# Gathered rows as three bfloat16 pieces, 88 blocks by matrix, and a round at every fourth step with four places left out

## The reference

```python
Xs = X[src]
msg = jnp.where((edge_types == 0)[:, None], Xs @ W_data.T + b_data, Xs @ W_control.T + b_control)
agg = jax.ops.segment_sum(msg, dst, num_segments=X.shape[0])
out = jax.nn.relu(agg + (X @ W_self.T + b_self))
result = _layernorm(x + out, axis=-1)      # all float32
```

## Time and profile before

| | us |
|---|---|
| median of 3 runs (3984.35 to 3987.94) | 3986.37 |
| the profiled execution | 3988.85 |
| its span on the core | 3987.1 |
| PE matmul busy | 2650.9 (66%) |
| POOL busy | 1715.3 (43%) |
| DVE busy | 1623.9 (41%) |
| ACT busy | 1267.6 (32%) |
| mean granted PE clock | 0.816 of full |

### The profile page before, as it was taken

The page is one execution under the profiler, slowest core; times in us unless marked ns, Lnnn a source line. Parts: engine busy times, 40 slices in busy tenths (PEclk is TensorE's granted clock), DMA queues, the critical chain, the costliest instruction groups (busy, mean ns, idle before and its releaser), DMA issues.

```text
span 3987.1 us, 50434 instructions
## 1 busy us (share of the span) xinstructions
PE 2650.9 (66%) x19115; PEld 1498.6 (38%) x19115; DVE 1623.9 (41%) x3683; ACT 1267.6 (32%) x2283; POOL 1715.3 (43%) x1815
## 2 busy tenths in 40 slices
PE   3566676666766677666666666667666666767666
PEld 2333343333433344333333334334333333333334
DVE  7434344334443344434344343434334343443332
ACT  4233232333323333333333333333333333323332
POOL 6434444344443444444344443444444344444432
PEclk9878788888887888888787888878888787888878
DMA  5111111111111111111111111111111111111110
GB/s 163 50 32 34 35 32 37 32 36 35 34 36 32 36 34 37 34 34 36 33 36 34 34 35 34 35 35 34 36 34 36 32 36 34 34 37 31 37 34 26
DMA packets 112877, 151.17 MB, mean 38 GB/s; under 512 B 35545, under 2 KB 82712, under 8 KB 112632
## 3 DMA queue, kind: packets, MB, share of 16 engines
q0 software_dynamic: 58432, 119.78, 11.4%
q1 hardware_dynamic: 54200, 28.09, 2.5%
HBM read 138.99 MB, written 8.76 MB: 37 GB/s over the span
## 4 chain that ended last, share of the span: by engine, by line
another core or an unknown queue 39%; PE 36%; ACT 17%; issue 6%; DVE 1%; DVEq 0%; DMA 0%; SPq 0%; ACTq 0%
PE apply_ps L615 20%; ACT cnt L799 15%; PE sum_ps L581 6%; PE build L599 5%; PE misc L664 2%; PE misc L667 1%; PE misc L665 1%; PE misc L666 1%; ACT sg L782 1%; ACT std L824 0%; ACT zg L784 0%; PE misc L558 0%; DVE cnt L1074 0%; DVE hot_q L1063 0%
## 5 line engine op out<-in xcount | busy, mean ns | idle before, releaser
L517 POOL DMA_INDIRECT rows<-in_x,src_t x1760 | 1670.9, 949 | 2195.0 <-PE sum_ps L581 1694.1
L615 PE MATMUL apply_ps<-x,cnt 128*128 128x385 bf16 x8428 | 1753.4, 364 | 10.4 <-issue 10.3
L799 ACT ACTIVATE cnt<-build 128x784 bf16<-128x784 f32 x1376 | 1060.9, 817 | 1878.0 <-remote 1586.2
L599 PE MATMUL build<-hot_q,hot_p 64*128 64x196 bf16 x5504 | 452.8, 274 | 1226.0 <-ACT cnt L799 1104.6
L615 PEld LDWEIGHTS apply_ps<-x,cnt 128*128 128x128 bf16 x8428 | 908.9, 110 | 686.9 <-issue 294.3
L599 PEld LDWEIGHTS build<-hot_q,hot_p 64*128 64x128 bf16 x5504 | 194.3, 97 | 1509.8 <-issue 1338.4
L1063 DVE TENSOR_TENSOR hot_q<-const_ps,key_pq 128x784 bf16<-128x784 f32 x688 | 663.4, 964 | 0.0
L1063 DVE TENSOR_TENSOR hot_p<-const_ps,key_pq 128x512 bf16<-128x512 f32 x688 | 468.4, 681 | 134.4 <-remote 108.5
L1135 DVE SCALAR_TENSOR_TENSOR y_sb<-misc,x_u 128x128 f32<-128x128 f32 (+2 forms) x104 | 30.3, 292 | 1057.4 <-PE misc L667 896.6
L1108 DVE TENSOR_TENSOR acc_deg<-misc,acc_deg 2x32 f32 x352 | 63.1, 179 | 927.5 <-PE misc L624 652.4
L782 ACT ACTIVATE sg<-sum_ps 128x129 f32<-128x129 f32 x176 | 49.0, 279 | 774.2 <-PE sum_ps L581 758.1
(11 more groups left out here) (174 smaller groups left out, 1063.5 us busy)
## 6 DMA issues: line engine op xcount, KB each, us to landing
rows<-in_x,src_t POOLq DMA_INDIRECT x1760
cnt<-in_x SPq DMA_DIRECT2D x13, 448.0 KB
x_u<-in_x SPq DMA_DIRECT2D x42, 64.0 KB
out<-out_sb SPq DMA_DIRECT2D x42, 64.0 KB
key_dram<-fin SPq DMA_DIRECT2D x12, 192.0 KB
x_u<-in_x SPq DMA_DIRECT2D x40, 53.5 KB
out<-out_sb SPq DMA_DIRECT2D x40, 53.5 KB
win_i<-in_dst SPq DMA_DIRECT2D x22, 64.0 KB, 2.0
```

The costliest lines, as they stand in the source:

```text
L517: pool.indirect_dma_start(out=rows[:, slot, 0:D], out_offset=None, in_=x, in_offset=bass.IndirectOffsetOnAxis(ap=src_t[:, col:col + 1], ax ...
L599: last = pe.matmul(build_ps[z][:, o:o + 2 * XBLOCKS], hot_p[half, slot, :], hot_q[half, slot, :], start=True, stop=True)
L615: last = pe.matmul(apply_ps[:, 0:385], cnt[:, k % 2, b, :], x3[:, b, 0:385], start=(b == 0), stop=(b == XBLOCKS - 1))
L799: act.activation(o, i.rearrange("p h (m b) -> p b h m", b=XBLOCKS), ACT.Copy).then_inc(evacuated, 1)
```

## The change

- `BLOCKS` goes from 86 to 88. 704 steps now build, where 688 did, and the last `apply` is in step 711. 1730 tiles are left to gather, which is 173 rounds.
- The rounds keep a grid of four steps, with 177 places, from step 0 to step 704. Places 23, 67, 111 and 155 have no round. The steps of the other jobs are now found by `place(s)`, which takes the next free step. So 70 of the units' outputs lie in the last step of a group of four (63 before), 24 turns of a unit's x lie there too (none before), and the loop ends 14 steps later.
- From round 12 (`F32_ROUNDS`) on, POOL gathers from a new DRAM tensor `x3_dram`, whose rows are the three bfloat16 pieces: 768 bytes instead of 512. PE adds them up with ten bfloat16 matmuls of 385 columns, one instruction each, and DVE adds the three pieces (`add_parts`), in place of ACT's `take_sums`.
- ACT's queue stores `x3` to `x3_dram` in steps 6 to 12, with 15 DMAs (`store_x3`).
- `AHEAD` goes from 3 to 2 rounds (`SLOTS` 20): the gathers of round r + 2 begin when round r is done.
- The last units have 88 rows instead of 128.

```diff
-BLOCKS = 86
+BLOCKS = 88
-GATHER_0 = 1365
+GATHER_0 = 1395
-SLOTS = 30
-AHEAD = 3
+SLOTS = 20
+F32_ROUNDS = 12
+ROW = 3 * D
+AHEAD = 2
...
+    places = (BATCHES + APPLY_AT) // 4 - (0 if BLOCKS == 86 else 1)
+    spare = places - PAIRS
+    left_out = {2 * ((places * (2 * i + 1) // (2 * spare)) // 2) + 1 for i in range(spare)}
+    gather_step = [4 * j for j in range(places) if j not in left_out][:PAIRS]
...
+    def place(s):
+        while s in taken:
+            s += 1
+        taken.add(s)
+        return s
+
+    sum_step = [place(s + 1) for s in gather_step]
+    key_step = {g: place(32 * g - 8) for g in range(1, KGROUPS)}
+    ptr_step = {g: place(8 if g == 1 else 32 * (g - 1)) for g in range(1, KGROUPS)}
+    block_step = [place(APPLY_AT + 8 * k + 10) for k in range(BLOCKS)]
...
+        x3_dram = nc.dram_tensor("x3_dram", [N, ROW], BF16).ap()
-        rows = sb("rows", [P, SLOTS, 132])
+        rows = sb("rows", [P, SLOTS, ROW + 2], BF16)
...
+                if ps == F32_ROUNDS:
+                    pool.wait_ge(x3_stored, 16 * (XCH + 1))
...
+                        out=rows_f[:, slot, 0:D] if early else rows[:, slot, 0:ROW],
+                        out_offset=None, in_=x if early else x3_dram,
...
-                    last = pe.matmul(sum_ps[64 * g:64 * g + 64, 0:D + 1], hot[:, ps % 3, g * GT + j, :],
-                                     rows[:, slot, 0:D + 1], start=(j == 0), stop=(j == GT - 1))
+                    part, st = slice(64 * g, 64 * g + 64), g * GT + j
+                    if ps < F32_ROUNDS:
+                        last = pe.matmul(sum_ps[part, 0:D + 1], hot[:, ps % 3, st, :], rows_f[:, slot, 0:D + 1],
+                                         start=(j == 0), stop=(j == GT - 1))
+                    else:
+                        last = pe.matmul(sum_ps[part, 0:ROW + 1], hot_b[:, ps % 3, st, :], rows[:, slot, 0:ROW + 1],
+                                         start=(j == 0), stop=(j == GT - 1))
...
+            def store_x3(c):
+
+                full = XB if c < XCH - 1 else XB - 1
+                act.wait_ge(x3_ready, c + 1)
+                act.dma_start(x3_dram[c * XB * P:(c * XB + full) * P, :].rearrange("(b p) d -> p b d", p=P),
+                              x3[:, c * XB:c * XB + full, 0:ROW]).then_inc(x3_stored, 16)
...
-                if q == 0 and ps < PAIRS:
-                    take_sums(ps)
+                if gather_at.get(s, PAIRS) < F32_ROUNDS:
+                    take_sums(gather_at[s])
...
+                for c in (2 * s - 12, 2 * s - 11):
+                    if 0 <= c < XCH:
+                        store_x3(c)
...
+            def add_parts(ps):
+
+                dve.wait_ge(rows_used, ps + 1)
+                dve.tensor_tensor(zg[:, ps % 2, :], t_mask[:, 0, :], sum_ps[:, ROW:ROW + 1].to_broadcast([P, 2]),
+                                  ALU.mult)
+                dve.tensor_reduce(sg[:, ps % 2, 0:D], sum_ps[:, 0:ROW].rearrange("p (k d) -> p d k", k=3), AX.X,
+                                  ALU.add).then_inc(sg_ready, 1)
```

More of the change, by code:

```diff
@@ L40 @@
 XB = 7
-TAIL = 4
 FIRST_X = 5
@@ L74, in gnn_resnorm @@
         cut = [n0 + (n1 - n0) * i // k for i in range(k + 1)]
+        end = sum_step[min(EPOCH * (e + 1), PAIRS) - 1]
         for i in range(k):
[L76 to L81, removed]
+            t, o = ((9, 10), (11, 15), (19, 23))[i]
+            wanted.append((end + t, Unit(cut[i], cut[i + 1] - cut[i], end + t, end + o, False, e % 2, cut[i] - base)))
+    tail_wanted = [w for w in wanted if w[1].n0 == DENSE - P or w[0] >= sum_step[-1] + 5 and not w[1].dense]
+    ends = [w[1] for w in tail_wanted]
+    TAIL = len(ends)
+    assert TAIL == 4 and ends[0].dense and not any(v.dense for v in ends[1:])
+    units = []
+    for s, v in sorted((w for w in wanted if w not in tail_wanted), key=lambda w: w[1].out):
+        s = place(max(s, units[-1].turn + 1 if units else 0))
+        units.append(v._replace(turn=s, out=place(max(s + 1, v.out, units[-1].out + 1 if units else 0))))
+    assert all(b.turn > a.out for a, b in zip(units, units[2:]))
     UNITS = len(units)
@@ L85, in gnn_resnorm @@
     assert len(turn_at) == UNITS and len(out_at) == UNITS
[L86 to L107, removed]
+    for v in units:
+        if not v.dense:
+            e = (v.n0 - WIN_0) // EPOCH_NODES
+            assert e + 2 >= EPOCHS or v.out + 2 < sum_step[EPOCH * (e + 2) - 1]
+        else:
+            u = v.n0 // P
+            assert v.out < block_step[min(2 * u + 4, BLOCKS - 1)]
+    TURN_END = BATCHES + 3
+    STEPS = max(taken) + 4
+    gather_at = {s: r for r, s in enumerate(gather_step)}
+    sums_at = {s: r for r, s in enumerate(sum_step)}.get
+    keys_at = {s: g for g, s in key_step.items()}.get
+    ptr_at = {s: g for g, s in ptr_step.items()}.get
+    block_turn_at = {s: k for k, s in enumerate(block_step)}.get
+    hot_at = {gather_step[r - 2] + 2: r for r in range(2, PAIRS)}
+    epoch_at = {sum_step[EPOCH * (e + 1) - 1] + 1: e for e in range(EPOCHS - 1)}
+    key_round = {min(r for r in range(PAIRS) if gather_step[r] >= s + (12 if g == 1 else 16)): g
+                 for g, s in ptr_step.items()}
     def posted_at(s):
@@ L137, in key_job @@
     def key_job(g):
-        return 1 if g == 0 else job[32 * g - 8]
+        return 1 if g == 0 else job[key_step[g]]
     def ptr_job(g):
-        return 0 if g == 0 else job[8 if g == 1 else 32 * (g - 1)]
+        return 0 if g == 0 else job[ptr_step[g]]
     ctx = ExitStack()
@@ L777, in split_mid @@
                 last.then_inc(mid_ready, 1)
+            def store_x3(c):
[3 more added lines that the diff above has]
+                              x3[:, c * XB:c * XB + full, 0:ROW]).then_inc(x3_stored, 16)
+                if full < XB:
+                    act.dma_start(x3_dram[(XBLOCKS - 1) * P:N, :], x3[0:XLAST, XBLOCKS - 1, 0:ROW]
+                                  ).then_inc(x3_stored, 16)
             def take_sums(ps):
@@ L874, in _ @@
                     act.wait_ge(end_turned, 1)
-                    act.activation(end_xt, build_ps[0][:, 0:TAIL * P].rearrange("p (j r) -> p j r", r=P),
-                                   ACT.Copy).then_inc(end_xt_ready, 1)
+                    for j, v in enumerate(ends):
+                        last = act.activation(end_xt[:, j, 0:v.r], build_ps[0][:, j * P:j * P + v.r], ACT.Copy)
+                    last.then_inc(end_xt_ready, 1)
             act.wait_ge(end_mv_ready, 1)
@@ L1193, in _ @@
                     post(posted_at(s))
+                if F32_ROUNDS <= gather_at.get(s, 0):
+                    add_parts(gather_at[s])
                 if sums_at(s) is not None:
```

115 lines of the change are left out of this document (67 added, 48 removed).

## The result

| | kernel before | changed kernel |
|---|---|---|
| median of 4 runs, us | 3986.89 (3984.35 to 3987.94) | 3943.68 (3940.96 to 3947.14) |
| ratio | 1 | 0.9894 (95%: 0.9882 to 0.9907) |
| span of the profiled execution, us | 3987.1 | 3939.8 |
| granted clock, mean | 0.816 | 0.825 |

The time fell by 43 us where the forecast was 12. The experiments then ran on three chips, and the kernel before took 3987, 3848 and 2310 us on them. They are called chips A, B and C here. The two kernels of the table ran beside each other, and as the kernel before took what it takes on A, they are counted to A. Times of kernels are compared only where both ran on the same chip.

A forecast was written before the change was run, and what follows sets the result against it. A serial loop through POOL, ACT and PE was taken as the bound, gathers holding back PE's signals to ACT. Terms +4 - 53 + 24 + 13 = -12 us gave 3974 us from 3986.4, 0.3% faster; range 3925 to 4070.

The forecast's parts named there:

- The frame: New schedule's beginning, held rounds, unheld round, left-out places and end, without the loop's own changes: together +4 us.
- Beginning, intervals and the unheld round: Round 5's sum at about 149: -13 us; one held interval fewer: -22.6; one more round without gathers behind it: +11.8.
- Left-out places: Four places without a round, each four steps with neither gathers nor sums, 10.5 us each: +42 us.
- The end: After the last sum, 19 us of applies and a 22 us finish, with the sum 42 us instead of 56.2: -14.
- The sums: PE's ten bfloat16 matmuls take 0.99 us instead of 1.32, -0.33 in each of 161 rounds: -53 us.
- the matmuls pair: Forecast: bfloat16 matmuls start in pairs on output halves. Rival: they don't, +80 instead of -53, 4107 us, chance 0.07.
- The larger gathers: 768-byte rows land later and release ACT later after POOL's last gather: +0.15 us a round, +24 us, bounds 0 and +48.
- ACT's freed 0.6 us: ACT's time freed by moving the sums' addition to DVE lies during POOL's gathers: no gain.
- The moved jobs: Seven more unit outputs behind the release, 1.86 us each: +13 us, bounds 0 and +25.
- The clock: Rival: PE's low clock after idling absorbs the loop's savings and costs, leaving only +4: 3990 us, chance 0.15.
- The larger transfers: Rival: larger gathers lengthen the hold of PE's signals by 0.7 us a round instead of 0.15: 4063 us, chance 0.10.
- let another step through: Rival: the hold catches another PE step; one more through, about 3590 us, one less, about 4380; chance 0.05 each.

The follow-up runs named there:

- the busy ACT: Changed kernel with ACT again waiting for the sums and running two small copies from round 12: 0.9965 of before on B, 2324.9 us (1.0065) on C.
- the kernel with float32 rows: Changed kernel, but all 173 rounds gather float32 rows and sum them with 20 float32 instructions: 4012.7 us on A, 1.0061 of before.
- the paced kernels: Changed kernel with waits added between POOL's gathers, all ten gathers kept: ratios to before from 0.7484 to 0.8784 on A and B, 1.1665 and 1.2827 on C.
- five gathers: Changed kernel, but from round 12 POOL gathers only five of ten sets of rows, each multiplied twice: 2652.7 us on A, 0.6651 of before.
- two bursts: Changed kernel, but POOL waits before the sixth gather until ACT has copied both halves of the third step's counts: 3162.4 us on A, 0.7931 of before.
- one each: Changed kernel, but from the third gather on each waits for one more half step's counts copied by ACT: 2982.5 us on A, 0.7484 of before.
- rows of three: Changed kernel, but POOL waits before every third gather until the previous one has landed: 3377.4 us on B, 0.8784 of before.

## Why the forecast was right in sign and short in size

**The bound.** The serial loop through POOL, ACT and PE was read rightly for this chip: on A, taking gathers away or breaking their row took 4.7 to 8.0 us out of each round with the same work on PE. That it is PE's signals that are late is borne out by the other waits: "remote" also ends waits of DVE for PE (122.9 us for `acc_deg` in the changed kernel), and none of PE's own. "If the hold were gone, PE's own steps would be next" is half shown on C: four steps take 12.56 us, where I had said 11.82, and POOL's 12.84 us a round stand beside them.

**The frame.** Beginning, intervals and the unheld round came within 2 us of their terms. Left-out places cost 11.4 us on average, not 10.5, as two of the four took 12.6. The end was -23 and not -14: after the last sums the applies took 19.6 us (I had 19), but the finish behind them 13.3 where I had carried 22 over from the earlier trace rows, which still held work of the last rounds.

**The sums.** Right: 1.01 us for ten, -53 in all, and the matmuls pair: 1.01 is 4 * 0.165 + 0.33 and a rounding, not 1.82. That rival is out.

**The larger gathers: the step that failed.** I had read from the earlier trace rows, a round that ends with key gathers, that 768 bytes release ACT 0.15 us later, and multiplied it by 161. On average the release comes 2.05 us after the last gather's end in the changed kernel, 2.02 in the same schedule with rows of 512 bytes, and 2.16 before (133, 133 and 137 rounds without key gathers). So the larger rows make a difference of 0.03 us there, and the 2.48 of that row wasn't the price of its bytes. One round is no price when the rows of 160 can be averaged. The landing did become later: the first event comes 2.34 us after a gather's start, 2.21 with 512 bytes, medians of over 1400 gathers each. The Trainium skill ("DMA: Bandwidth & Descriptors", Anatomy of one DMA, SWDGE path) fits a transfer with a fixed time and its bytes at 436 GB/s; an estimate by this page is 0.075 us more for the added 32 KB, and the trace has 0.13. But no one on the path waits for a landing here, and so neither figure belongs into the sum. Without this term, and with the finish at 13, the forecast would have been -12 - 24 - 9 = -45. That this is what was measured is luck: the lost pairs (+12) and the dearer places and unheld round (+5) had no term, and the 17 us that the gathers and moved jobs came out below +13 cancel them.

**ACT's freed 0.6 us.** I put them at nothing, as they lie beside the gathers. Between 13 and 27 us of the gain may be theirs or the clock's (the experiment with the busy ACT leaves it open; the traces lean to the clock).

**The moved jobs.** +13 forecast, +14 read from the kernel with float32 rows, but as a sum of +30 and -16.

**The rivals.** The clock didn't take the loop's savings back: float32 rows cost 69 us, more than the 53 of the sums. The larger transfers didn't lengthen the hold. No round let another step through more often; on the contrary, the pairs of the earlier trace rows were lost, 12 us which no term of mine had. The beginning was at 148.89, so x3's stores didn't press on it.

**What no rival had.** Each one was a number on the same chip. On C, where nothing is held, the same change makes the kernel 0.7% slower (1.0054 to 1.0081). An estimate for it from the lines above: 161 * 0.33 = 53 us less of sums, and 16 more steps of at least 2.5 us, 40 to 47 us more, comes out at about even; the measured +16 isn't explained, as no trace of the kernel before exists from C.

## What to carry to other kernels

Where an engine's wait has no releaser in the trace, ask which other engine's activity starts and ends with it, and break that activity up before tuning around it: one added wait a round in POOL's queue was worth 20%, eight were worth 24% of the changed kernel's time, where the whole change was worth 1.1%. Take a price from the mean over all its occurrences, not from the one row that shows it best. And before such a wait is kept, run both kernels on another chip: the paced kernels took 12 to 25% less time than the kernel before on A and B, while on C pacing cost 17 to 28% (by other waits than on A and B), and the unpaced kernel before was the fastest of all.

## What the runs showed of the hardware that I hadn't expected

- **A hold of PE's signals by gathers, on some chips only.** The kernel before took 3987.2 us on A, 3847.9 on B (13 runs, 3834.9 to 3857.1) and 2309.7 on C (9 runs, 2308.8 to 2310.8). Of the `build` signals to ACT from the 61st on, 164 of 1348 came over 3 us late in the changed kernel on A (168 of 1316 before), and none over 1 us late on C.
- **When it begins and ends.** In the kernels on A with unbroken rows of ten, signals raised up to 3.5 us after a row's first gather went through, and those from 5.3 us on were held (163 to 165 in each kernel); hardly any fall between. In "five gathers", "two bursts" and "one each" all but two of the held ones were raised after 3.6 us, and none after 4.6 us went through at once. The fourth gather of a row starts at 3.76 us. The release comes later behind a longer row: 1.1 us after the last of four gathers, 1.4 of five, 1.5 of six and 2.1 to 2.2 of ten (medians). A row of three doesn't start the hold: in that kernel 5 of 1348 signals were over 1 us late. An interruption of 1.7 us between two gathers mostly ends it.
- **The trace itself is thinner where signals are held.** It holds 9194 landing events of DMAs in the kernel before and 8801 in the changed one on A, 20896 with rows of three on B, and 31101 for the changed kernel on C, though from the changed kernel on the DMAs are the same. So the path that carries such events may be what is congested; that is a guess. The Trainium skill ("NOTIFIC — Programmer's Manual", 1.1 The problem) says of the recording of events: "The engine never blocks on the host". Its section 1.2 (The design, and what it trades) names modes in which a full ring loses records or stalls the producer. The missing events would fit the first of these; whether recording has a part in the hold, no run here shows, since all of them were recorded.
- **A landing has a beginning and an end.** A gather's first event comes at 2.34 us, but a wait for all sixteen ends 2.90 to 2.92 us after its start on B. A price for waiting on it is the second.
